# Three weight slots, regrouped output tiles and other PSUM banks in a fused mixer and MoE layer on eight cores

## The reference

```python
# mixer
xn = rms_scale * x / (norm(x) * D**-0.5 + EPS) * split_scale      # x is layernormed before
K = sigmoid(xn @ W_K)
u, g_in, g_out = split(xn @ W_ugg, 3)                             # 2048 features each
u = u * sigmoid(g_in) * (1 - K)
h = scan(h[t] = K[t-1] * h[t-1] + u[t])                           # over the tokens
y = (h * sigmoid(g_out)) @ W_out + x
x1 = x_in + layernorm(y)
# 32 experts, 8 per token, and one shared expert
z = layernorm(x1)
w = top8 weights of sigmoid(z @ gate_w.T), by groups
routed = sum_e w[:, e] * (silu(z @ Wg_e.T) * (z @ Wu_e.T)) @ Wd_e.T
shared = (silu(z @ Sg.T) * (z @ Su.T)) @ Sd.T
out = x1 + layernorm(routed + shared)
```

## Time and profile before

| | |
|---|---|
| median of 3 runs | 5859.22 us |
| lowest and highest | 5626.87 and 6239.28 us |
| the profiled execution | 5629.84 us, span of its slowest core 5628.0 us |
| spans of the eight cores in it | 5604.8 to 5628.0 us, clock 0.885 to 0.886 |
| TensorE busy | 4193.0 us, 75% |
| VectorE busy | 2449.4 us, 44% |
| ScalarE busy | 1023.6 us, 18% |

### The profile page before, as it was taken

One profiled execution on the slowest core, in us unless ns is written; L12 is line 12 of the kernel. 1 busy time (PEld: TensorE's weight loads), 2 busy tenths in 40 slices (PEclk: granted clock), 3 DMA queues, 4 the chain that ended last, 5 costly groups with the idle time before them and its releaser, 6 DMA issues.

```text
span 5628.0 us, 51917 instructions; the slowest of 8 cores (5604.8 to 5628.0 us)
## 1 busy us (share of the span) xinstructions
PE 4193.0 (75%) x16942; PEld 1661.2 (30%) x16942; DVE 2449.4 (44%) x3805; ACT 1023.6 (18%) x1286; POOL 108.5 (2%) x171
## 2 busy tenths in 40 slices
PE   1367870666537999999999995438999999999993
PEld 1123330211112333333333332113333333333331
DVE  6134431444542444444444444433444444444444
ACT  3134430211122111111111111222111111111111
POOL 0111120000000000000000000000000000000000
PEclk9788985777768999999999997669999999999996
DMA  2999999992103323333233320113323333233310
GB/s 61 106 123 115 116 113 119 121 122 40 23 0 60 68 53 60 68 68 61 52 68 68 68 53 15 37 23 60 68 53 61 68 68 61 52 68 68 68 30 30
DMA packets 922229, 370.49 MB, mean 66 GB/s; under 512 B 910484, under 2 KB 910484, under 8 KB 918710
## 3 DMA queue, kind: packets, MB, share of 16 engines
q1 hardware_dynamic: 848502, 239.24, 21.1%
q0 software_dynamic: 73472, 127.94, 20.1%
HBM read 272.77 MB, written 115.34 MB: 69 GB/s over the span
## 4 chain that ended last, share of the span: by engine, by line
PE 69%; DVE 11%; DMA 6%; issue 4%; another core or an unknown queue 4%; ACT 4%; SPq 1%; DVEq 0%; POOL 0%; ACTq 0%; POOLq 0%
PE pf L1135 17%; PE pf L1180 17%; PE pf L1145 16%; DMA wub<-wugg 5%; PE py L700 2%; PE pj L500 2%; PE pj L563 1%; PE pj L508 1%; PE pj L528 1%; PE pf L1116 1%; PE pf L1025 1%; PE pf L1056 1%; PE pf L1117 1%; PE pf L1029 1%
## 5 line engine op out<-in xcount | busy, mean ns | idle before, releaser
L1180 PE MATMUL pf<-act,edT 128*128 128x512 bf16 x4096 | 971.4, 378 | 205.7 <-DVE act L1167 118.6
L1135 PE MATMUL pf<-ln2b,egT 128*128 128x512 bf16 x4096 | 991.7, 404 | 22.9 <-DMA euT<-eu_st 22.9
L1145 PE MATMUL pf<-ln2b,euT 128*128 128x512 bf16 x4096 | 904.9, 379 | 0.0
L1189 DVE TENSOR_TENSOR routed<-routed,pf 128x512 f32<-128x512 f32 x1024 | 704.1, 688 | 427.3 <-PE pf L1180 426.4
L1163 DVE TENSOR_TENSOR sgl<-sgl,pf 128x512 f32<-128x512 f32 x512 | 352.3, 688 | 1135.8 <-PE pf L1145 1135.8
L1156 ACT ACT_TABLE_LOAD x128 | 164.2, 1283 | 2493.5 <-PE pf L1135 2493.5
L1135 PEld LDWEIGHTS pf<-ln2b,egT 128*128 128x128 bf16 x4096 | 416.8, 103 | 608.0 <-issue 190.2
L1180 PEld LDWEIGHTS pf<-act,edT 128*128 128x128 bf16 x4096 | 342.0, 96 | 835.1 <-issue 545.7
L1145 PEld LDWEIGHTS pf<-ln2b,euT 128*128 128x128 bf16 x4096 | 400.7, 98 | 483.4
L1167 DVE TENSOR_TENSOR act<-sgl,wrep 128x512 bf16<-128x512 f32 x512 | 354.5, 692 | 54.7 <-DVE sgl L1163 1.8
L1156 ACT ACTIVATE sgl<-pf 128x512 f32<-128x512 f32 x512 | 295.5, 596 | 297.9 <-PE pf L1135 295.2
(11 more groups left out here) (203 smaller groups left out, 2809.7 us busy)
## 6 DMA issues: line engine op xcount, KB each, us to landing
eg_st<-eg POOLq DMA_DIRECT2D x32, 1024.0 KB, 99.3
eu_st<-eu POOLq DMA_DIRECT2D x32, 1024.0 KB, 108.8
ed_st<-ed POOLq DMA_DIRECT2D x32, 1024.0 KB, 119.6
wub<-wugg POOLq DMA_DIRECT2D x48, 256.0 KB, 28.5
x<-x SPq DMA_DIRECT2D x4, 2048.0 KB, 9.6
x2b<-x SPq DMA_DIRECT2D x4, 2048.0 KB, 199.7
out<-outtm SPq DMA_DIRECT2D x4, 2048.0 KB, 7.1
wkb<-wk POOLq DMA_DIRECT2D x16, 256.0 KB, 14.4
```

The costliest lines, as they stand in the source:

```text
L1135: last = t.matmul(pf[ic][:, :], egT[slot][:, dc, ic * 128:(ic + 1) * 128], ln2b[:, dc, tt * 512:(tt + 1) * 512], start=(dc == 0), stop=(dc ...
L1145: last = t.matmul(pf[4 + ic][:, :], euT[slot][:, dc, ic * 128:(ic + 1) * 128], ln2b[:, dc, tt * 512:(tt + 1) * 512], start=(dc == 0), stop ...
L1180: last = t.matmul(pda[:, :], edT1[:, ic, dc * 128:(dc + 1) * 128], act[:, ic, tt, :], start=(ic == 0), stop=(ic == 3))
L1189: iv = inc(v.tensor_tensor(routed[:, dc, tt * 512:(tt + 1) * 512], routed[:, dc, tt * 512:(tt + 1) * 512], pda[:, :], ALU.add), "cv")
```

## The change

Three places are edited.

1. Projections: three weight slots in place of two, each with its semaphore; the copies of expert hc/2 are ordered in even blocks only, so that eight experts are ordered in the loop and 24 behind it. The buffer name `xn` becomes four names, one per group of tokens.
2. Mixer output: two `xf_sb`. The body of the loop over tiles is divided into functions and called in another order: the load, transposes and copies of the next tile are issued between the sums of the block output and the `row_finalize` behind them, the squares of the next tile behind the last additions, and the sums of x (L671 before) behind the squares.
3. Experts: the spread weights go to pf0 and pf1, the first of the two matmuls raises the semaphore too, and the second copy waits for the first.

```diff
-            wkb = [... for i in range(2)]
-            wub = [... for i in range(2)]
+            wkb = [... for i in range(3)]
+            wub = [... for i in range(3)]
...
-                slot = hc % 2
+                slot = hc % 3
...
-                    for e in (hc,):
+                    if hc % 2 == 0:
+                        e = hc // 2
                         inc(g.dma_start(eg_st[e], eg_d[e]), "ss", 16)
                         inc(g.dma_start(eu_st[e], eu_d[e]), "ss", 16)
                         inc(g.dma_start(ed_st[e], ed_d[e]), "ss", 16)
...
-                        pre(t, "t", reads=("xn", wsl), writes=(f"pj{tt}",))
+                        pre(t, "t", reads=(f"xn{tt}", wsl), writes=(f"pj{tt}",))
...
-                for e in range(HCN, NE):
+                for e in range(HCN // 2, NE):
...
-            xf_sb = s2.enter_context(nc.sbuf_tensor("xf_sb", [128, DC, 512], F32))
+            xf_sb2 = [s2.enter_context(nc.sbuf_tensor(f"xf_sb{i}", [128, DC, 512], F32)) for i in range(2)]
...
+            a2_load(0)
+            a2_trans(0)
+            a2_sq(0)
+            for tt in range(NT):
+                a2_xstatmm(tt)
+                a2_y(0, tt)
+                a2_y(1, tt)
+                a2_xfin_bc1(tt)
+                a2_bo(0, tt)
+                a2_bo(1, tt)
+                for dc in range(2, DC):
+                    a2_y(dc, tt)
+                    a2_bo(dc, tt)
+                a2_bostats(tt)
+                if tt + 1 < NT:
+                    a2_load(tt + 1)
+                    a2_trans(tt + 1)
+                a2_bofin_bc2_x1(tt)
+                if tt + 1 < NT:
+                    a2_sq(tt + 1)
...
-                        pre(t, "t", reads=("sele", "wfm"), writes=("pf4", "pf5"))
-                        t.matmul(pf[4][:, :], sel_ee[:, :], w_fm[:, 0:512], start=True, stop=True)
-                        it = inc(t.matmul(pf[5][:, :], sel_ee[:, :], w_fm[:, 512:1024],
+                        pre(t, "t", reads=("sele", "wfm"), writes=("pf0", "pf1"))
+                        inc(t.matmul(pf[0][:, :], sel_ee[:, :], w_fm[:, 0:512], start=True, stop=True), "ct")
+                        it = inc(t.matmul(pf[1][:, :], sel_ee[:, :], w_fm[:, 512:1024],
                                           start=True, stop=True), "ct")
-                        post("ct", it, reads=("sele", "wfm"), writes=("pf4", "pf5"))
+                        post("ct", it, reads=("sele", "wfm"), writes=("pf0", "pf1"))
...
-                        pre(v, "v", reads=("pf4", "pf5"), writes=("wrepsb",))
-                        v.tensor_copy(wrep_sb[:, 0, :], pf[4][:, :])
-                        iv = inc(v.tensor_copy(wrep_sb[:, 1, :], pf[5][:, :]), "cv")
-                        post("cv", iv, reads=("pf4", "pf5"), writes=("wrepsb",))
+                        pre(v, "v", reads=("pf0", "pf1"), writes=("wrepsb",))
+                        iv = inc(v.tensor_copy(wrep_sb[:, 0, :], pf[0][:, :]), "cv")
+                        wt(v, "v", [("cv", iv)])
+                        iv = inc(v.tensor_copy(wrep_sb[:, 1, :], pf[1][:, :]), "cv")
+                        post("cv", iv, reads=("pf0", "pf1"), writes=("wrepsb",))
```

More of the change, by code:

```diff
@@ L75, in build @@
     cnt = {}
-    for name in ("ct", "cv", "cs", "cg", "syc", "sx0", "sx1", "sgw0", "sgw1", "sgo",
+    for name in ("ct", "cv", "cs", "cg", "syc", "sx0", "sx1", "sgw0", "sgw1", "sgw2", "sgo",
                  "ss", "ss2", "st0", "st1", "st2", "st3", "so", "sdbg"):
@@ L445, in _ @@
                 def _(g):
-                    pre(g, "g", reads=("xn",))
-                    post("sdbg", inc(g.dma_start(dbg["xn"], xn_fm[:, :, :]), "sdbg", 16), reads=("xn",))
+                    pre(g, "g", reads=("xn0", "xn1", "xn2", "xn3"))
+                    post("sdbg", inc(g.dma_start(dbg["xn"], xn_fm[:, :, :]), "sdbg", 16), reads=("xn0", "xn1", "xn2", "xn3"))
             barrier()
@@ L453, in build @@
             pj = [s1.enter_context(nc.psum_tensor(f"pj{i}", [128, 512], F32)) for i in range(8)]
-            wkb = [s1.enter_context(nc.sbuf_tensor(f"wkb{i}", [128, 8, 128], BF16)) for i in range(2)]
-            wub = [s1.enter_context(nc.sbuf_tensor(f"wub{i}", [128, 8, 3, 128], BF16)) for i in range(2)]
+            wkb = [s1.enter_context(nc.sbuf_tensor(f"wkb{i}", [128, 8, 128], BF16)) for i in range(3)]
+            wub = [s1.enter_context(nc.sbuf_tensor(f"wub{i}", [128, 8, 3, 128], BF16)) for i in range(3)]
             K_sb = s1.enter_context(nc.sbuf_tensor("K_sb", [128, S], F32))
@@ L636, in build, with a2_load @@
             r1r = s2.enter_context(nc.sbuf_tensor("r1r", [1, 512], F32))
-            for tt in range(NT):
+            def a2_load(tt):
                 xs = f"x2b{tt % 2}"
@@ L661, in _, with a2_sq @@
                     def _(s, tt=tt, dc=dc, pxb=pxb):
[L662 to L674, removed]
+                        pre(s, "s", reads=(pxb,), writes=(f"xf{tt % 2}",))
+                        ic_ = inc(s.copy(xf_sb2[tt % 2][:, dc, :], pxT[dc % 2][:, :]), "cs")
+                        post("cs", ic_, reads=(pxb,), writes=(f"xf{tt % 2}",))
+            def a2_sq(tt):
                 for dc in range(DC):
@@ L691, in _ @@
                         res["prow2"].w["ct"] = cnt["ct"]
[L693 to L720, removed]
@@ L722, in build, with a2_xstatmm, _ @@
-                a2_y(0)
-                a2_y(1)
+            def a2_xstatmm(tt):
+                @block.tensor
+                def _(t, tt=tt):
+                    pre(t, "t", reads=(f"xf{tt % 2}", "ones128"), writes=("prow1",))
+                    for dc in range(DC):
+                        last1 = t.matmul(prow1[0:1, :], ones128[:, :], xf_sb2[tt % 2][:, dc, :],
+                                         start=(dc == 0), stop=(dc == DC - 1))
+                    it1 = inc(last1, "ct")
+                    post("ct", it1, reads=(f"xf{tt % 2}", "ones128"), writes=("prow1",))
@@ new lines, in a2_y, with _ @@
+            def a2_y(dc, tt):
+                pyb = f"py{dc % 2}"
+                @block.tensor
+                def _(t, tt=tt, dc=dc, pyb=pyb):
+                    pre(t, "t", reads=("woutsb", AR[tt]), writes=(pyb,))
+                    for hcb in range(HCN):
+                        last = t.matmul(py[dc % 2][:, :], wout_sb[:, hcb, dc * 128:(dc + 1) * 128],
+                                        gated_ap(hcb, tt), start=(hcb == 0), stop=(hcb == HCN - 1))
+                    it2 = inc(last, "ct")
+                    post("ct", it2, reads=("woutsb", AR[tt]), writes=(pyb,))
@@ L724, in build, with a2_xfin_bc1 @@
+            def a2_xfin_bc1(tt):
                 row_finalize(prow1[0:1, :], prow2[0:1, :], "prow1", "prow2", DM)
@@ L739, in _, with a2_bostats @@
                     post("ct", it, reads=("mu1r", "onesc"), writes=("pmu", "prr"))
[L741 to L745, removed]
+            def a2_bostats(tt):
                 @block.tensor
```

57 lines of the change are left out of this document (37 added, 20 removed).

## The result

The changed kernel takes 6083.07 us in the median of nine executions (5697.08 to 6239.73); the kernel before, over ten, 5705.03 us (5622.84 to 6289.3). In seven of those nine executions and five of those ten the cores of one die, or of both, are granted a lower TensorE clock than in the profiled one (0.77 to 0.87 in place of 0.88) and the time is 3 to 12% longer, so the comparison goes by the other executions: the ratio is 1.0178, 95% interval 1.0101 to 1.0255. A second measurement of the same two kernels (`after_again`) gave 1.0112 (1.006 to 1.0164), and core by core the two profiled executions are 1.0 to 1.4% apart. The change makes this kernel slower by 1 to 2%. A difference of 2% is what counts here as a change; the first interval reaches past it, the second does not.

What follows compares the result with a forecast made beforehand. It took DMA to bound the projections, a chain of engines the output stage and TensorE the experts: 5629.8 - 134 (projections) + 12 (output) + 120 (expert stall) + 53 (clock) = 5681 us, range 5595 to 5765.

Steps and rivals of the forecast that it cites:

- The footing: Whole time: forecast from the profiled execution, 5629.8 us, which stands by the lowest of three times, 3.9% under the median.
- Projections: -134: Projections: with copies in every second block, TensorE binds the blocks after the start; stage ends at 728 instead of 862 us.
- The third slot: Projections: weights ordered two blocks ahead, so the queue's 50 us per two blocks fit TensorE's 58.
- The cover of the copies: Expert copies: last lands by 1375 us, SyncE needs them about 1666; 290 us of cover, cost nothing.
- The names xn0 to xn3 give nothing: Projections: the four buffer names bring no gain, since a barrier stands between the stages.
- Output: +12: Output stage: copies hold up ScalarE's root and x is late once; 12 us slower, ends -10 and +25.
- rival E: Output stage: the root isn't held and the transposes vanish; 5622 us, same; 5%.
- Experts: +173: Experts: TensorE stalls 1.87 us per expert behind the copies, 120 us, and loses 53 us to the clock.
- A: Experts: copies are hidden and gate products don't wait; 5508 us, faster by 2.2%; 5%.
- C: Experts: clock loses two stretches per expert, 109 us rather than 53; 5757 us, slower by 2.3%; 14%.
- D: Projections: small pieces make weights dearer, blocks stay DMA-bound at about 33 us; 51 us less gain, 5732 us; 8%.
- B: Experts: the stall is there but the clock suffers no more than now; 5628 us, same; 17%.

Runs made afterwards that it cites:

- s2: Kernel before with the new buffer names and an expert's copies in even blocks only, but two weight slots; projections 564.5 us.
- n1: Changed kernel with the four buffer names xn0 to xn3 called xg0 to xg3; input stage 144.8 us instead of 152.8.
- o1: Output-stage edit alone, second row_finalize and its broadcast issued before the next tile's load and transposes; output stage 588.9 us.
- b1: Experts edit alone, weight row in banks 2 and 3, each gate bank waited for only where needed; experts 3846.1 us.
- c1: Experts edit alone plus eight unused products per expert into bank 4 while the copies run; experts 3928.8 us against 4023.1.
- x1: Kernel before with two selector tiles, the next expert's made ahead of the down products; experts 3680.1 us, span 5444.3.

## Why the prediction was right and wrong

- **The footing failed.** "I predict on its footing", the profiled execution by the lowest of three, is the step that put the time out of the range. The median is 6083, 402 us above the forecast. The sum accounts for 16 of them: the changed kernel's own profiled execution took 5697. The other 386 lie between that execution and the median, which is of an execution with one die at a clock of 0.80, and the sum has no term for them. Two of the three times shown stood 4 and 11% above the profiled one, so a range around 5681 that ended at 5765 left no room. Nor does the median belong to the kernel alone: `after_again` gave 5796.8 over seven executions, 286 us less for the same kernel. What lowers the clock in some executions is open; no run here shows it.
- **The sum, and some luck in it.** In sign and size the argument holds: 5681 is 0.9% above the profiled execution before, and the ratios measured are 1.0112 and 1.0178. But part of the agreement is luck. On core 2 the parts came to +54.2 us for +51; the projections and the output stage were 16 us better than forecast, the experts and the names 19 worse.
- **Projections: -134, measured -147** (134 to 147 less by core). The mechanism is as said: TensorE binds from block 4 on. The two starting steps were 40.4 and 33.4 us for 42.3 and 38.1, the period 28.9 for 29.1. The largest miss is block 3's step: its weights were there 4.7 us sooner than an expert and a block's weights at the old pace. The waits for weights fell to 94.9 us, not 130.
- **The third slot.** "Weights ordered two blocks ahead, so the 50 of 58 can be used" is refuted by `s2`: two slots give 564.5. With the copies thinned, two slots use the 50 of 58 as well as three.
- **The cover of the copies.** Right. They end by 1375 us (the DMA share falls from 1.01 to 0.37 between 1360 and 1372), expert 0 is ordered at 1658, and no expert waits for them.
- **"The names xn0 to xn3 give nothing."** Wrong by 7.5 us. I looked for what the new names release, and not for what they collide with. `n1` shows it.
- **Output: +12, measured +8.6** (5 to 9 by core; 3.4 on core 2 in `after_again`). The parts are right one by one: x late by 17.95 us (17.0 forecast), the root behind the copies, tile 1's squares 65.8 us after the sums (17.0 + 47.9). `o1` settles rival E: the 15.7 us per tile are there to be had, and it is the order on ScalarE that withholds them. The prediction took the 16.8 us of transposes and copies as given; 10.3 of them are table loads, see the last section.
- **Experts: +173, measured +184.7** (185 to 195 by core). The stall is 1.96 us (121.7 over 62) for 1.87: +125 for +120. The rest is 60 for 53: a gate product takes 487.0/1915 = 254.3 ns instead of 242.7, 48 us over 4096 of them, the clock's part (0.95); the wait ahead of the row is 0.12 us longer, 8 us; 4 are left. `b1` shows the stall gone once products for other banks stand ahead of the wait; `c1` and `x1` show that the idle time costs clock beside itself, and how much.
- **Rivals.** A fell with the stall, C with 60 for its 109, D with 28.9 us steps, E as above. B fell with the gate products' 254.3 ns and the clock of 0.95, and again in `c1`. The Trainium skill, "TensorE: Matmul & The Clock Gate", section "Loop structure matters more than you think", says that a VectorE copy out of PSUM does not break TensorE's warmth. Here filling that copy's 1.95 us gave 116 us back. The page's example lets the next products follow immediately; these waited for the copy, and the measurement decides.

## What to carry to other kernels

Where TensorE stands between two dense groups, look at what the wait names, not only at how long it is: here a wait that asked for four banks when one would do cost its own 1.95 us per expert (125 us) and more than a third as much again in clock (48 us). Moving work "under" another engine's work helps only if no queue in between carries something the critical chain needs first; on an in-order engine the short item goes ahead of the long one. And before taking a profiled execution as the time to be forecast, set the range by how far the times shown spread, for both kernels.

## What the runs showed of the hardware

- With a wait of 1.13 us ahead of each expert's weight row, part of the gate products behind it ran at the lower clock level (mean of one 405 ns, clock of the stretch 0.97); without it, in `x1`, they did not (379 ns, 0.99).
- A plain copy on ScalarE costs 0.58 us, and in `a2_trans` each brings a table load of 1.28 us with it, so that one starts every 1.96 us and the eight take 15.7 us, 10.3 of them in table loads. ScalarE's timeline in the changed kernel, core 2:

```profile
958.59 1.28 ACT L665 ACT_TABLE_LOAD   x1
959.88 0.58 ACT L665 COPY xf_sb<-pxT 128x512 f32<-128x512 f32 x1
```

- These loads follow the kernel's text and not a change of function. At the lines looked at, each `@block.scalar` section, a stretch of the program given to ScalarE, opens with one. In the kernel before, the 64 sigmoids of L538 stand in sections of one and have 64 loads, the 64 of L518 in sections of four and have 16 (core 2):

```profile
L538 ACT ACT_TABLE_LOAD  x64: 1283/1283/1283, 178.2 to 848.7; - x64
L518 ACT ACT_TABLE_LOAD  x16: 1283/1283/1283, 164.1 to 826.1; - x16
```

  One section for a tile's eight copies should so save up to 7 x 1.28 = 9 us per tile, an estimate from these rows; no run tries it.

- A transposing load from SyncE, 5.6 us in issue as a rule, was held 238.87 us while GpSimd's DRAM-to-DRAM copies filled the engines; before the change the same copies held nothing (5.95 us), since they ended ahead of it.
